# Normalising and storing the output rows beside the last expert's products, with the last expert's rows patched afterwards

## The reference

```python
x = x + xattn(layernorm(x), ctx)                  # 16 heads, 77 keys
h = layernorm(x)                                  # the rows that are routed
gates, idx = top_k(softmax(h @ wg), 2)            # two of eight experts for each token, capacity 1280
y = silu(disp @ fc1_w.T + fc1_b) @ fc2_w + fc2_b  # each expert on its rows: 256 -> 1024 -> 256
res = h + sum(gates * y of the token's two experts)
out = x + layernorm(res) * ln_gamma + ln_beta
```

## Time and profile before

| what | us |
|---|---|
| median of 3 runs (lowest, highest) | 763.94 (763.0, 767.59) |
| the profiled execution's own time | 763.03 |
| its span, first to last instruction | 761.3 |
| TensorE / VectorE / ScalarE / GpSimd busy | 672.8 / 551.4 / 409.8 / 419.7 |
| mean granted TensorE clock | 0.94 |

### The profile page before, as it was taken

One profiled execution on the slowest core, in us unless ns is written; L12 is line 12 of the kernel. 1 busy time (PEld: TensorE's weight loads), 2 busy tenths in 40 slices (PEclk: granted clock), 3 DMA queues, 4 the chain that ended last, 5 costly groups with the idle time before them and its releaser, 6 DMA issues.

```text
span 761.3 us, 15549 instructions
## 1 busy us (share of the span) xinstructions
PE 672.8 (88%) x5562; PEld 643.6 (85%) x5562; DVE 551.4 (72%) x1129; ACT 409.8 (54%) x956; POOL 419.7 (55%) x541
## 2 busy tenths in 40 slices
PE   4999999999999645999999999999999999999500
PEld 3799999999988534999999998999999999999500
DVE  6578888888888795766566689687696566855187
ACT  6355555555555583545445475555555455634185
POOL 5445665665663426254544668576585653631456
PEclk9699999999999956999999999999999999999855
DMA  9710111111101124244334346453555342322474
GB/s 295 208 37 31 43 37 35 43 35 37 43 30 43 42 76 140 72 98 100 55 93 106 57 106 123 110 111 59 113 114 113 74 78 47 59 33 24 71 261 152
DMA packets 61348, 64.81 MB, mean 85 GB/s; under 512 B 15057, under 2 KB 56529, under 8 KB 61137
## 3 DMA queue, kind: packets, MB, share of 16 engines
q1 hardware_dynamic: 45201, 42.35, 17.7%
q0 software_dynamic: 15360, 21.31, 17.3%
q10 hardware_dynamic: 704, 0.01, 0.0%
HBM read 39.22 MB, written 23.72 MB: 83 GB/s over the span
## 4 chain that ended last, share of the span: by engine, by line
PE 84%; DVE 8%; DMA 3%; issue 2%; POOL 1%; ACT 1%; POOLq 0%; SPq 0%; DVEq 0%; ACTq 0%
PE banks L918 19%; PE banks L920 19%; PE banks L919 18%; PE banks L1054 8%; PE banks L1040 6%; PE banks L1028 5%; PE banks L1181 2%; DMA sum_rows<-y_sb,slot_ids 2%; PE banks L1090 1%; PE banks L941 1%; PE banks L963 1%; DVE oh_lo L1495 1%; DVE oh_id L1491 1%; DMA res<-sum_rows 1%; DVE z L1734 1%
## 5 line engine op out<-in xcount | busy, mean ns | idle before, releaser
L633 POOL DMA_INDIRECT sum_rows<-y_sb,slot_ids x80 | 131.0, 1638 | 164.0 <-ACT y_sb L861 147.5
L871 ACT ACTIVATE hraw<-banks,b_now 128x256 f32<-128x256 f32 x320 | 132.2, 476 | 90.1 <-PE banks L920 89.9
L918 PE MATMUL banks<-xT_hi,w_hi 128*128 128x256 f32 x560 | 161.8, 289 | 1.7 <-ACT xT_hi L843 1.7
L920 PE MATMUL banks<-xT_hi,w_lo 128*128 128x256 f32 x560 | 158.8, 284 | 0.0
L919 PE MATMUL banks<-xT_lo,w_hi 128*128 128x256 f32 x560 | 158.5, 283 | 0.0
L918 PE MATMUL banks<-w_hi,h_hi 128*128 128x256 f32 x528 | 149.0, 282 | 2.4 <-issue 1.6
L919 PE MATMUL banks<-w_lo,h_hi 128*128 128x256 f32 x528 | 148.7, 282 | 0.0
L920 PE MATMUL banks<-w_hi,h_lo 128*128 128x256 f32 x528 | 148.6, 281 | 0.0
L1700 DVE TENSOR_TENSOR h_lo<-hraw,h_hi 128x512 fp32r<-128x512 f32 x160 | 113.4, 709 | 5.5
L1698 DVE CAST h_hi<-hraw 128x512 fp32r<-128x512 f32 x160 | 79.4, 496 | 44.9 <-ACT hraw L871 44.2
L918 PEld LDWEIGHTS banks<-xT_hi,w_hi 128*128 128x128 f32 x560 | 106.5, 190 | 2.1 <-issue 2.1
(11 more groups left out here) (218 smaller groups left out, 1392.9 us busy)
## 6 DMA issues: line engine op xcount, KB each, us to landing
w1raw<-in_w1T SPq DMA_DIRECT2D x8, 1024.0 KB, 6.9
w2raw<-in_w SPq DMA_DIRECT2D x8, 1024.0 KB, 6.8
xn_rows<-xn SPq DMA_DIRECT2D x32, 128.0 KB, 1.7
sum_rows<-xn SPq DMA_DIRECT2D x32, 128.0 KB, 1.8
out<-z SPq DMA_DIRECT2D x16, 256.0 KB, 2.2
res<-sum_rows SPq DMA_DIRECT2D x7, 512.0 KB, 8.4
X<-in_x SPq DMA_DIRECT2D x2, 1280.0 KB, 12.5
xg<-xn_rows,slot_ids POOLq DMA_INDIRECT x80, 3.8
```

What stands on the lines that cost most here:

```text
L633: g.indirect_dma_start(sum_rows, bass.IndirectOffsetOnAxis(ap=slot_ids[:, st, 1, q:q + 1], axis=0), y_sb[:, u, q, :], None, bounds_check=N ...
L871: a.activation(hraw[:, j // 2, j % 2, :], banks[:, j // 2, (j % 2) * 256:(j % 2 + 1) * 256], ACT.Silu, bias=b1_now[:, (c // SPE) % 2, j:j ...
L918: t_.matmul(o, a_hi, b_hi, start=first, stop=False)
L920: return t_.matmul(o, a_lo, b_hi, start=False, stop=last)
```

## The change

In the new kernel the sums of seven experts are normalised and stored while the eighth is computed, and the eighth expert's rows are done again afterwards.

- `sum_rows` becomes half of `sum_both`, a table whose row holds the sum (256 floats) and beside it the residual row, `X` with beta added. The residual rows are stored during the experts, four tiles at a time. Scatters use doubled row numbers (`sum_ids`).
- The first seven experts (steps 0 to 34, `SL` = 35) scatter as before. Then SyncE loads the sums of all tiles into buffers that are free by then (`wave`), the loads of tile 8 on behind the first four gathers; GpSimd gathers for each of the eighth expert's ten blocks of 128 slots the row of `sum_both` (sum and residual, 2 KB a row) with one indirect DMA (`gather_sums`).
- The eight quads are begun in three steps of the last expert: quads 0 and 1 in step 36, 2 to 4 in step 37, 5 to 7 in step 38 (`QUADS_OF_STEP`); their later parts follow one and two steps on. VectorE makes the statistics of two tiles by one instruction and finishes one tile of the quad; ScalarE normalises the other three, GpSimd multiplies them by gamma, VectorE adds `X`. SyncE stores a quad by one DMA.
- In the last expert the cast `h_hi` goes from VectorE to ScalarE (`activation_hi`); `b2` is added by two matmuls with one row of weights in each half; VectorE's `patch_sum` multiplies the product by the gate and adds it to the gathered sum, in place of the addition of `b2`, ScalarE's scaling and the scatter.
- At the end the ten blocks are normalised by VectorE (`patch_begun`, `patch_done`) with GpSimd's power, and GpSimd scatters them to `out` with plain indirect DMAs, after all eight stores of quads have landed.

```diff
-    sum_rows = nc.dram_tensor("sum_rows", [N + 4 * P, D], f32, kind="Internal").ap()
+    sum_both = nc.dram_tensor("sum_both", [N + 4 * P, 2 * D], f32, kind="Internal").ap()
+    sum_rows = sum_both.rearrange("n (a d) -> (n a) d", a=2)
+    both_t = sum_both[0:N, :].rearrange("(t p) (a d) -> p t a d", p=P, a=2)
+    sum_t, rest_t = both_t[:, :, 0, :], both_t[:, :, 1, :]
...
+        LAST = NE - 1
+        SL = LAST * SPE
+        FREE = 1 - LAST % 2
+        EARLY_SUMS = 2
+        QUADS_OF_STEP = {SL + 1: (0, 1), SL + 2: (2, 3, 4), SL + 3: (5, 6, 7)}
...
+        spare = [flat(w1raw[:]), w2raw[:]] + [late_rows[:, 8 * n:8 * n + 8, :] for n in range(4)]
+
+        def wave(a, b):
+
+            return spare[a // 8][:, a % 8:a % 8 + b - a, :]
...
+            sp.wait_ge(sem("beta_added"), NT)
+            sp.dma_start(rest_t[:, NT - QT:NT, :], X[:, NT - QT:NT, 0:D]).then_inc(rests_stored, 16)
+
+            for u in range(2):
+                sp.wait_ge(scattered[u], 32 * ((SL + 1 - u) // 2))
+            sp.wait_ge(sem("w_hi_made"), 4 * NE)
+            sp.wait_ge(sem("w_lo_made"), 4 * NE)
 
 
             for n, (a, b) in enumerate(RES_LOADS):
-                sp.dma_start(res[:, a:b, :], sum_t[:, a:b, :]).then_inc(load_res[n], 16)
-            for g, a in enumerate(halves_in_order()):
-                sp.wait_ge(sem("out_made"), g + 1)
-                sp.dma_start(out_t[:, a:a + 2, :], z[:, a:a + 2, :]).then_inc(stored, 16)
-            sp.wait_ge(stored, 16 * (NT // 2))
+                if a == 2 * QT:
+                    sp.wait_ge(sums_gathered[0], 16 * 2 * EARLY_SUMS)
+                sp.dma_start(wave(a, b), sum_t[:, a:b, :]).then_inc(load_res[n], 16)
+            for k in range(NQ):
+                sp.wait_ge(sem("out_made"), k + 1)
+                sp.dma_start(out_t[:, QT * k:QT * (k + 1), :], wave(QT * k, QT * (k + 1))).then_inc(stored, 16)
+            sp.wait_ge(stored, 16 * NQ)
+            sp.wait_ge(patched, 16 * 2 * SPE)
 
 
         @block.gpsimd
...
+                if within(st, SL):
...
-                        g.indirect_dma_start(sum_rows, bass.IndirectOffsetOnAxis(ap=slot_ids[:, st, 1, q:q + 1], axis=0),
-                                             y_sb[:, u, q, :], None, bounds_check=N + 4 * P - 1, oob_is_err=False,
+                        g.indirect_dma_start(sum_rows, bass.IndirectOffsetOnAxis(ap=sum_ids[:, st, q:q + 1], axis=0),
+                                             y_sb[:, u, q, :], None, bounds_check=2 * (N + 4 * P) - 1, oob_is_err=False,
                                              compute_op=ALU.add).then_inc(scattered[u], 16)
+
+            def gather_sums(m):
+                for q in range(2):
+                    g.indirect_dma_start(gathered_row(2 * m + q), None, sum_both[0:N, :],
+                                         bass.IndirectOffsetOnAxis(ap=slot_ids[:, SL + m, 0, q:q + 1], axis=0),
+                                         bounds_check=N - 1, oob_is_err=False).then_inc(sums_gathered[m >= EARLY_SUMS], 16)
...
+            def first_scaled(k):
+                for n in range(QT - 1):
+                    pool.wait_ge(sem("z_made"), (QT - 1) * k + n + 1)
+                    z = row_of(wave(QT * k + n, QT * k + n + 1))
+                    g.tensor_tensor(z, z, gamma_sb[:], ALU.mult).then_inc(sem("z_scaled"), 1)
...
+            def scatter_patch(m):
+                for q in range(2):
+                    n = 2 * m + q
+                    pool.wait_ge(sem("out_made"), NQ + n + 1)
+                    g.indirect_dma_start(out, bass.IndirectOffsetOnAxis(ap=slot_ids[:, SL + m, 1, q:q + 1], axis=0),
+                                         patch(n), None, bounds_check=N - 1, oob_is_err=False)\
+                        .then_inc(patched, 16)
+
+            for u in range(2):
+                pool.wait_ge(scattered[u], 32 * ((SL + 1 - u) // 2))
+            pool.wait_ge(rests_stored, 16 * NQ)
+            for m in range(EARLY_SUMS):
+                gather_sums(m)
+            deviations(0)
+            deviations(1)
+            gather_sums(EARLY_SUMS)
+            for k in (2, 3, 4):
+                deviations(k)
+            first_scaled(0)
+            first_scaled(1)
+            for m in range(EARLY_SUMS + 1, SPE):
+                gather_sums(m)
+            for k in (5, 6, 7):
+                deviations(k)
+            for k in range(2, NQ):
+                first_scaled(k)
+            patch_deviations(0)
+            patch_deviations(1)
+            pool.wait_ge(stored, 16 * NQ)
+            for m in range(SPE):
+                scatter_patch(m)
+                patch_deviations(m + 2)
 
...
+            def activation_hi(c, n):
+
+                if n == 0:
+                    act.wait_ge(sem("fc2_done"), c - 1)
+                act.wait_ge(sem("h_made"), HJ * c + 2 * n + 2)
+                a.activation(h_hi[:, c % 2, 2 * n:2 * n + 2, :], hraw[:, n], ACT.Copy).then_inc(sem("last_hi_made"), 1)
+
+            def first_normalised(k):
+
+                act.wait_ge(sem("nmr_made"), k + 1)
+                for t in range(QT * k, QT * (k + 1) - 1):
+                    z = row_of(wave(t, t + 1))
+                    a.activation(z, z, ACT.Identity, scale=rstd_d[:, t:t + 1], bias=nmr_d[:, t:t + 1])\
+                        .then_inc(sem("z_made"), 1)
 
...
+                if c in (SL, SL + 1):
+                    scale_results(c - 2)
...
+                        if st >= SL and j % 2 and j > 1:
+                            activation_hi(st, j // 2 - 1)
+                    if st >= SL:
+                        activation_hi(st, HJ // 2 - 1)
+                if c not in (SL, SL + 1):
+                    scale_results(c - 2)
+                e, s = c // SPE + 1, c % SPE
                 if s and within(e, NE):
                     split_quarter(e, (c // SPE + 1) % 2, s - 1)
+                for k in QUADS_OF_STEP.get(c - 1, ()):
+                    first_normalised(k)
 
             expert_steps(act, expert_step)
-
...
+                        if e == LAST:
+                            pe.wait_ge(sem("bias_split"), 3)
+                            for n in range(2):
+                                t_.matmul(o, ones_r[:], b2_r[:, n, :], start=(n == 0), stop=False)
...
+            then(v.tensor_copy(sum_f[:], slot_ids[:, :, 1, :]))
+            v.tensor_scalar(sum_ids[:], sum_f[:], 2.0, 0.0, ALU.mult, ALU.max).then_inc(sem("ids_made"), 1)
...
+            def pair_stats(n):
+                t = 2 * n
+                res_loaded(dve, t)
+                v.bn_stats(st_d[:, n].rearrange("p a b -> p (a b)"), wave(t, t + 2).rearrange("p t d -> p d t"))\
+                    .then_inc(sem("st3_made"), 1)
+
+            def quad_begun(k):
+
+                a = QT * k
+                for n in (2 * k + 1, 2 * k):
+                    pair_stats(n)
+                dve.wait_ge(sem("st3_made"), 2 * k + 2)
+                v.tensor_scalar(var_d[:, a:a + QT].rearrange("p (a b) -> p a b", b=2), st_d[:, 2 * k:2 * k + 2, :, 2],
+                                1.0 / D, EPS_LN, ALU.mult, ALU.add).then_inc(sem("var3_made"), 1)
+                t = a + QT - 1
+                z = row_of(wave(t, t + 1))
+                v.scalar_tensor_tensor(z, z, st_d[:, t // 2, 1, 1:2], gamma_sb[:], ALU.subtract, ALU.mult)\
+                    .then_inc(sem("z_scaled_dve"), 1)
...
+            def first_bias(k):
+                a = QT * k
+                dve.wait_ge(sem("rstd3_made"), k + 1)
+                v.scalar_tensor_tensor(nmr_d[:, a:a + QT].rearrange("p (a b) -> p a b", b=2), st_d[:, 2 * k:2 * k + 2, :, 1],
+                                       -1.0, rstd_d[:, a:a + QT].rearrange("p (a b) -> p a b", b=2), ALU.mult, ALU.mult).then_inc(sem("nmr_made"), 1)
...
+            def last_done(k):
+                t = QT * (k + 1) - 1
+                dve.wait_ge(sem("rstd3_made"), k + 1)
+                dve.wait_ge(sem("z_scaled_dve"), k + 1)
+                z = row_of(wave(t, t + 1))
+                v.scalar_tensor_tensor(z, z, rstd_d[:, t:t + 1], X[:, t, 0:D], ALU.mult, ALU.add)
+
+            def first_done(k):
+                a = QT * k
+                dve.wait_ge(sem("z_scaled"), (QT - 1) * (k + 1))
+                z = row_of(wave(a + 2, a + 3))
+                v.tensor_tensor(z, z, X[:, a + 2, 0:D], ALU.add)
+                v.tensor_tensor(wave(a, a + 2), wave(a, a + 2), X[:, a:a + 2, 0:D], ALU.add).then_inc(sem("out_made"), 1)
+
+            def patch_sum(c):
+
+                if c == SL:
+                    dve.wait_ge(sums_gathered[0], 16 * 2 * EARLY_SUMS)
+                if c == SL + EARLY_SUMS:
+                    dve.wait_ge(sums_gathered[1], 16 * 2 * (SPE - EARLY_SUMS))
+                for q in range(2):
+                    dve.wait_ge(sem("fc2_done" if q else "fc2_half_done"), c + 1)
+                    r = patch(2 * (c - SL) + q)
+                    v.scalar_tensor_tensor(r, banks[:, YB + q, 0:D], xg[:, c % XR, q, D + LAST:D + LAST + 1], r,
```

(46 more changed lines are left out.)

206 lines of the change are left out of this document (87 added, 119 removed).

## The result

| kernel | median of runs (lowest, highest), us | ratio to before, 95% interval |
|---|---|---|
| before, on the chips of all runs | 763.9 to 765.8 | |
| changed | 771.14 (768.18, 772.13), 6 runs | 1.0084 [1.0056, 1.0111] |
| changed, measured again with the experiments | 772.21 (770.26, 773.59), 4 runs | 1.0104 [1.0079, 1.0128] |

The forecast was 757 with a range to 767: the changed kernel is about 1% slower, not 0.9% faster. The profiled execution took 771.7 us, its span is 770.0.

What follows compares the result with a forecast made beforehand. TensorE was taken as the bound, with VectorE's quads behind its last product. That stretch shrinks 14 us, TensorE gives back 8.1 (2.3 bias, 5.8 waits): span 6.0 us less, 757 us, range 749 to 767.

Steps and rivals of the forecast that it cites:

- What bounds the kernel now: Whole span: TensorE bounds, then 46.6 us behind the last product; steps have 6.1, 7.2 and 8.9 us of room on three engines.
- What stays in place: Before the last expert: storing residual rows costs 0; doubled row numbers 0 to 0.5 us, taken as 0.
- The bias matmuls: Last expert on TensorE: 20 more matmuls at 0.117 us each, 2.3 us; bounds 0 and twice that.
- When the quads can begin: After step 34: first loads arrive at 675.9 us, and the last of four gathers lands at 681.5.
- First wait: Step 37's patch_sum(35) waits for gathers, so fc2(36) begins 1.8 us late; 0.9 to about 4.
- The quads in VectorE's queue: Steps 37 and 38: VectorE has 14 us against 12.3; patch_sum(37) waits for gathers, delaying fc2(38) by 0.8 us.
- The wait that costs most: Before fc2(39): patch_sum(38) queues behind first_done(4), which waits for GpSimd's multiplications at 0.85 us each; cost 3.2 us.
- Behind the last product: The end: TensorE ends at 722.6 us; last quads, stores and ten scatters at 1.39 us follow, ending at 755.3.
- B: Last expert and end: GpSimd is the bound through slower multiplications and scatters; 765 us, up to 768; chance 0.19.
- C: Wait before fc2(39): TensorE's clock falls, 52 matmuls take 0.23 us, 6 us more; time 763; chance 0.14.

Runs made afterwards that it cites:

- E8: Changed kernel with the two bias matmuls given 128 rows of weights (one of ones, the others zero), nothing else; 768.93 us, 1.0045.
- E1: Changed kernel with first_bias moved from VectorE to ScalarE, as four small operations a quad; 772.01 us, 1.0096.
- E2: Changed kernel without GpSimd's 24 multiplications by gamma, so 24 of 32 output tiles lack gamma; 759.41 us, 0.9932.
- E5: Changed kernel with GpSimd waiting for the biases before multiplying, and first_done of quads 2 to 4 behind patch_sum(38); 760.47 us, 0.9942.
- E7: E5 with 128-row bias matmuls, three pairs' statistics ahead of the last patch_sum and all powers ahead of the stores; 760.93 us, 0.9952.
- E9: E5 with 128-row bias matmuls, and first_done(5), one patched pair's statistics and first_done(6) ahead of the last patch_sum; 760.59 us, 0.9943.
- E12: The changed kernel, unaltered, measured once more beside the others on the same chip; 772.21 us.
- E4: Changed kernel with first_done of quads 2 to 4 moved behind patch_sum(38) in VectorE's order; 765.27 us, 1.0003.
- E10: Changed kernel with first_bias as three 128 x 1 operations, each with one tensor and one scalar per partition; 774.76 us, 1.0144.
- E3: Changed kernel with one added wait: GpSimd multiplies quads 2 to 7 only when all eight biases are made; 768.26 us, 1.0038.
- E15: E9 with patch_sum(35) behind two gathers alone, quad_begun(1) behind it, and GpSimd's last four gathers ahead of quads 0 and 1; 761.84 us, 0.9962.
- E17: Changed kernel with GpSimd's six gathers together and its multiplications of quads 2 and 3 ahead of quads 5 to 7's powers; 772.97 us, 1.0116.

## Why the prediction was wrong

It put the last product 8.1 us later and the stretch behind it 14 us shorter. The second half held, the first was 15 us short.

- **What bounds the kernel now**: the room on VectorE and GpSimd was read right (5.9 and 3.1 us of 12), but taken as the sum of two engines that do not disturb each other. It is not: 10.9 and 10.9.
- **What stays in place**: 0, measured 1.15 us ahead of the last expert.
- **The bias matmuls**: mechanism right, size wrong. 2.3 us by the interval of 128-row matmuls; 6.2 measured, even above my upper bound of 4.7. The shape was in no row of before, and the bound from the nearest row was too narrow. E8, 2.2 to 3.3 us faster for 3.8 less on TensorE, shows that more than half of this was on the path.
- **When the quads can begin**: gathers landed at 683.3, predicted 681.5, of which 1.15 is the shift. Right.
- **First wait** and **The quads in VectorE's queue**: the first two waits together are 2.8 us, predicted 2.6. Right in the profiled execution; the clock, not foreseen there, fell in the first wait or within 1 us behind it in E1, E2, E5 to E7, E9 and E12 (waits of 1.5 to 2.6 us), and did not in the changed kernel's first profile (1.4) or E8 (1.7).
- **The wait that costs most**: this is the step that failed. Right place, engine and line; 3.2 us predicted, 10.1 measured; but not what the line waited behind. I had VectorE stand in `first_done(4)` until GpSimd had multiplied the tiles of quads 2 to 4, at 714.9. They were ready at 716.5, of which 1.15 is the shift, and VectorE never waited for one: it came to `first_done(2)` at 722.6 only, since its own operations took longer. GpSimd was given a price for contention (0.85; it is 0.99 shared), VectorE none: low parts at 0.66 (measured 0.68 alone, 1.22 shared), pair additions at 0.62 (1.21), and a bias at 0.15 that was held for 5.2. Rows 13 showed both sides slowed, and I applied only one. E2 is the measure: without the multiplications the same list takes 7.6 us, not 16.3.
- **Behind the last product**: predicted 32.7 us (722.6 to 755.3), measured 31.9. GpSimd's first scatter begins 11.5 us behind TensorE's end (predicted 11.6), a plain scatter's start-to-start is 1.28 to 1.5 us (1.39), the last one's start to the end of the span 6.0 (5.0).

With the right sizes the sum is 1.15 + 3.9 + 7.1 (waits 12.9, not 5.8) + 3.1 (clock) - 0.8 = 14.5 us above the forecast; the profiled execution is 14.7 above it.

Of the **rivals**, B's time was nearest and its mechanism half right: GpSimd's multiplications, but through what they do to VectorE rather than through their own length, which was 0.70 us each for the nine ahead of `first_done(4)`. C's mechanism came true as well, at 3.1 us instead of 6, since the clock is back some 6 us after the matmuls resume (0.82 in the window of 734 to 736). I had made them alternatives; the long wait brings the low clock, so they add up.

The Trainium skill, "SBUF — State Buffer", section Who interferes with whom, says that the shared port pair is an exclusive lock, not a throttle, and that issue order decides who blocks. The held operations (5.2 and 10.95 us) agree in that VectorE's stood still, but the section has the pair held for one instruction, and the 10.95 us span some fifteen multiplications in a row; here the measurement decides. The stretches in which both run at 1.0 to 1.2 us look like turns taken operation by operation. I had used this page for a price per multiplication, where its weight lay on VectorE's side.

**What stays open.** Whether a stretch shares or locks: held operations began 1.1 to 2.0 us behind GpSimd's first multiplication in the changed kernel, E4, E8 and E10, and shared ones within 0.3 us of it in E1, E3 and E12; but in E10 at 695.4, 1.5 us behind it, they shared, and in E15 a bias that began 0.05 us behind it (695.43, 695.38) was held for 3.5 us. No run isolates this. Why E1's median is 772 when its one profile shows 765.3 is open too. So is what would take the good versions below 760 us. E2, which has neither cure, reaches 759.4; that the sharing is the limit of the others too is an inference from E17's rows; no version without these multiplications on GpSimd, but with gamma, was run.

## What to carry to other kernels

Room on VectorE and room on GpSimd is not two rooms if both would read two tensors from SBUF: charge each such GpSimd operation to VectorE as well (here 0.5 us for each of 0.7), and in the worst case VectorE stands still until GpSimd pauses. An operation that TensorE waits for should stand ahead of work that TensorE does not need; putting one such reading first and letting GpSimd start behind the short operations (E5) turned 1% slower into 0.6% faster. Where a kernel has many queues in balance, removing a wait that the trace shows moves it more often than it removes it: none of the seven versions made from E5 is more than 1.4 us from its time.
